# First expert weights loaded slot by slot through SyncE's queue, rectification moved to ScalarE

## The reference

```python
x = L0_attn_x
x = x + _L0_attn_ref(_layernorm(x, axis=-1), Wq, Wk, Wv, Wo, bo)
x = x + _L0_ffn_ref(_layernorm(x, axis=-1), gate_w, w1, b1, w2, b2)

def _L0_ffn_ref(x, gate_w, w1, b1, w2, b2):
    logits = x_flat @ gate_w.T
    probs = jax.nn.softmax(logits / TEMPERATURE, axis=-1)
    topk_probs, topk_idx = jax.lax.top_k(probs, TOPK)          # TOPK = 2
    hidden = jax.nn.relu(jnp.einsum('th,ehf->tef', x_flat, w1) + b1[None])
    all_out = jnp.einsum('tef,efh->teh', hidden, w2) + b2[None]
    gathered = jnp.take_along_axis(all_out, topk_idx[:, :, None], axis=1)
    y_flat = jnp.sum(gathered * topk_probs[:, :, None], axis=1)
```

## Time and profile before

| | us |
|---|---|
| median of 3 runs | 551.57 |
| lowest, highest | 549.81, 553.23 |
| the profiled execution's own time | 548.82 |
| its span, first to last instruction | 547.0 |
| its mean granted TensorE clock | 0.958 |

### The profile page before, as it was taken

The page is one execution under the profiler, slowest core; times in us unless marked ns, Lnnn a source line. Parts: engine busy times, 40 slices in busy tenths (PEclk is TensorE's granted clock), DMA queues, the critical chain, the costliest instruction groups (busy, mean ns, idle before and its releaser), DMA issues.

```text
span 547.0 us, 14291 instructions
## 1 busy us (share of the span) xinstructions
PE 473.8 (87%) x4081; PEld 328.4 (60%) x4081; DVE 415.6 (76%) x1538; ACT 361.6 (66%) x786; POOL 288.5 (53%) x583
## 2 busy tenths in 40 slices
PE   2788999999999999999998899868977889998880
PEld 1534556645546545545545455337867789998870
DVE  5888788998888988988979889725767445556784
ACT  8564877767867867867866668745663467776640
POOL 4512444454766755765765755673454555553441
PEclk9857999999999999999999999998997999999995
DMA  7333233233243243243233236621122222227353
GB/s 217 111 92 107 83 86 103 65 103 98 69 117 102 70 119 105 65 122 103 66 120 101 71 100 168 181 74 51 55 69 69 79 65 71 70 71 253 96 151 96
DMA packets 49741, 54.92 MB, mean 100 GB/s; under 512 B 6851, under 2 KB 41841, under 8 KB 49664
## 3 DMA queue, kind: packets, MB, share of 16 engines
q1 hardware_dynamic: 45312, 45.44, 29.5%
q0 software_dynamic: 4320, 8.47, 4.5%
q10 hardware_dynamic: 32, 0.10, 0.0%
HBM read 34.96 MB, written 17.90 MB: 97 GB/s over the span
## 4 chain that ended last, share of the span: by engine, by line
PE 48%; DVE 29%; issue 8%; ACT 5%; DMA 4%; another core or an unknown queue 2%; SPq 1%; POOL 1%; DVEq 0%; ACTq 0%; POOLq 0%
PE psO L991 11%; DVE psS L1300 11%; PE psS L961 7%; PE psT L1149 7%; DVE maxs L1303 6%; PE psM L1160 5%; PE psO L1160 4%; PE psT L974 3%; PE psS L1149 2%; DVE maxs L1300 2%; PE psS L1139 1%; DMA xs_t<-sorted_x 1%; DVE xn L1230 1%; PE psS L964 1%
## 5 line engine op out<-in xcount | busy, mean ns | idle before, releaser
L774 ACT ACTIVATE PT<-psT 128x512 f32<-128x512 f32 x320 | 172.6, 594 | 71.7 <-PE psO L991 47.0
L1300 DVE CUSTOM_DVE_ANT_0 psS<-mask_row,psS 128x512 f32<-128x512 bf16 (+1 forms) x256 | 157.0, 626 | 36.1 <-PE psS L961 32.8
L961 PE MATMUL psS<-Ks,Qs 96*128 96x128 bf16 (+3 forms) x512 | 135.7, 314 | 13.5 <-DVE maxs L1303 7.5
L581 POOL TENSOR_SCALAR_AFFINE_SELECT PT<-PT 128x512 f32<-128x512 f32 x128 | 79.3, 634 | 106.2 <-ACT PT L774 105.1
L659 POOL DMA_INDIRECT token_y<-Qs,y_row x71 | 70.8, 997 | 83.8 <-DVE Qs L1638 49.7
L974 PE MATMUL psT<-Qs,Ks 108*128 108x384 bf16 (+3 forms) x512 | 110.2, 302 | 3.5 <-ACT PT L774 2.7
L961 PEld LDWEIGHTS psS<-Ks,Qs 96*128 96x128 bf16 x512 | 50.8, 100 | 60.7 <-DVE maxs L1303 24.6
L991 PE MATMUL psO<-PT,Vs 128*32 128x512 f32 (+3 forms) x1024 | 76.0, 436 | 0.9 <-DVE x_all L1326 0.7
L608 POOL DMA_INDIRECT sorted_x<-xn,place x64 | 64.0, 999 | 18.8 <-issue 17.2
L1303 DVE TENSOR_REDUCE maxs<-psS 128x2 f32<-128x512 f32 (+1 forms) x96 | 62.9, 682 | 2.2 <-PE psS L964 1.4
L858 ACT ACTIVATE krest<-psT,turned 128x128 f32<-128x128 f32 x142 | 44.2, 363 | 30.4 <-PE psT L1149 12.0
(11 more groups left out here) (255 smaller groups left out, 744.8 us busy)
## 6 DMA issues: line engine op xcount, KB each, us to landing
Qs<-q_parts SPq DMA_DIRECT2D x96, 96.0 KB
Ks<-k_parts SPq DMA_DIRECT2D x95, 96.0 KB
xs_t<-sorted_x SPq DMA_DIRECT2D x71, 65.0 KB
w_sb<-in_L_ffn_w SPq DMA_DIRECT2D x16, 256.0 KB
q_parts<-qparts SPq DMA_DIRECT2D x32, 96.0 KB, 2.4
k_parts<-kparts SPq DMA_DIRECT2D x8, 384.0 KB, 2.6
x_all<-in_L_attn_x SPq DMA_DIRECT2D x8, 256.0 KB, 4.6
v_all<-token_y SPq DMA_DIRECT2D x4, 512.0 KB, 4.2
```

What stands on the lines that cost most here:

```text
L581: pool.affine_select(out=square, in_=square, compare_op=ALU.is_ge, fill=0.0, base=0, pattern=[[0, GH], [1, P]], channel_multiplier=-1).the ...
L774: act.activation(PT[:, n * T:(n + 1) * T], psT[:, bank, :], ACT.Exp).then_inc(prob_done[bank], 1)
L961: last = pe.matmul(psS[:, bank, c0:c0 + n], Qs[0:QK_ROWS, g, h, j * P:n], Ks[0:QK_ROWS, g, h, 0:n], start=True, stop=alone)
L1300: dve.tensor_tensor_reduce(src, mask_row[:, (CH - 1 - j) * P:], src, 1.0, NEG, ALU.add, ALU.max, maxs[:, par, j, h:h + 1]).then_inc(scores ...
```

## The change

- `load_w1(i, at)` is new on SyncE. It loads 128 x 512 of w1 for slot i from the input in device memory straight to the slot's buffer, 256 KB, once `h_ready` shows that the slot that had the buffer was expanded. SyncE gets an `expert_reader` of its own. The loop issues it for slot i+5, ahead of the load of xs for slot i+6.
- `w1_t` is a ring of four: two halves of `qrest` and the two of `xn`. `w1_sb` and its 8 loads during attention are gone, and `moe_in` counts 9 DMAs instead of 17. `expand(i)` waits for the slot's own `w1_loaded` instead of ScalarE's `w1_copied`.
- `copy_w1` on ScalarE is gone. ScalarE rectifies all four pieces of a slot. VectorE's `relu` is gone.
- From slot 26 on SyncE waits for the second routing (`routed` at 2) before a w1 load.
- The stores of finished batches come one slot later, at slots 57, 60, 63, 66 and 69.

```diff
-STORES = [SLOT_ENDS[0] + 9, SLOT_ENDS[0] + 12, SLOT_ENDS[0] + 15, SLOT_ENDS[0] + 18, SLOT_ENDS[0] + 21]
+STORES = [SLOT_ENDS[0] + 10 + 3 * b for b in range(SORTED[0])]
...
-        w1_sb = sb("w1_sb", [P, E, F])
...
-        w1_t = qrest
+        w1_t = [qrest[:, 0, :], qrest[:, 1, :]] + [xn[:, n, :, :].rearrange("p c d -> p (c d)") for n in range(2)]
...
             def load_experts(experts):
                 for e in experts:
-                    sp.dma_start(w1_sb[:, e:e + 1, :].rearrange("p a f -> p (a f)"), w1[e]).then_inc(moe_in, 16)
...
+            def load_w1(i, at):
+
+                at_least(sp, h_ready, i - ROUND + 1)
+                sp.dma_start(w1_t[i % ROUND], w1[bass.ds(expert_of(i, at), 1), :, :].rearrange("a d f -> d (a f)"))\
+                    .then_inc(w1_loaded[i % ROUND], 16)
...
-            for i in range(AHEAD):
+            expert_of = expert_reader(sp)
+            for i in range(ROUND):
                 load(i)
+                load_w1(i, 0)
+            load(ROUND)
+            load_w1(ROUND, 0)
+            load(ROUND + 1)
             stored = 0
             for i in range(NSLOTS):
+                if i + ROUND + 1 < NSLOTS:
+                    if (i + 2) // ROUND == ROUNDS0[1]:
+                        sp.wait_ge(routed, 2)
+                    load_w1(i + ROUND + 1, i + 2)
                 if i + AHEAD < NSLOTS:
                     load(i + AHEAD)
...
-            def copy_w1(i, e):
-
-                at_least(act, h_ready, i - 1)
-                act.activation(w1_t[:, i % 2, :], w1_sb[:, bass.ds(e, 1), :].rearrange("p a f -> p (a f)"), ACT.Copy)\
-                    .then_inc(w1_copied, 1)
-
             def relu(i, e):
 
                 act.wait_ge(h_ready, i + 1)
                 at_least(act, y_ready, i - 1)
-                for c in range(FC // 2):
-                    last = act.activation(hT[:, i % 2, c * P:(c + 1) * P], banks[2 * (i % 2)][:, c * P:(c + 1) * P], ACT.Relu,
+                for c in range(FC):
+                    bank, c0 = banks[2 * (i % 2) + c // (FC // 2)], c % (FC // 2) * P
+                    last = act.activation(hT[:, i % 2, c * P:(c + 1) * P], bank[:, c0:c0 + P], ACT.Relu,
                                           bias=b1T[:, bass.ds(e * FC + c, 1)])
-                last.then_inc(relu_act, 1)
+                last.then_inc(relu_done, 1)
...
                 pe.wait_ge(xsT_copied, i + 1)
-                pe.wait_ge(w1_copied, i + 1)
-                at_least(pe, relu_act, i - 1)
-                at_least(pe, relu_dve, i - 1)
+                pe.wait_ge(w1_loaded[i % ROUND], (i // ROUND + 1) * 16)
+                at_least(pe, relu_done, i - 1)
...
-            def relu(i, e):
-
-                dve.wait_ge(h_ready, i + 1)
-                at_least(dve, y_ready, i - 1)
-                for c in range(FC // 2, FC):
-                    c0 = (c - FC // 2) * P
-                    last = dve.tensor_scalar(hT[:, i % 2, c * P:(c + 1) * P], banks[2 * (i % 2) + 1][:, c0:c0 + P],
-                                             b1T[:, bass.ds(e * FC + c, 1)], 0.0, ALU.add, ALU.max)
-                last.then_inc(relu_dve, 1)
```

More of the change, by code:

```diff
@@ L313, in layer @@
         results_loaded = sems("results_loaded", BATCH)
-        row_found, xs_loaded = sem("row_found"), sems("xs_loaded", ROUND)
-        xs_turned, xsT_copied, w1_copied, h_ready, relu_act, relu_dve, y_ready, y_copied = (
-            sem(n) for n in ("xs_turned", "xsT_copied", "w1_copied", "h_ready", "relu_act", "relu_dve", "y_ready", "y_copied"))
+        row_found, xs_loaded, w1_loaded = sem("row_found"), sems("xs_loaded", ROUND), sems("w1_loaded", ROUND)
+        xs_turned, xsT_copied, h_ready, relu_done, y_ready, y_copied = (
+            sem(n) for n in ("xs_turned", "xsT_copied", "h_ready", "relu_done", "y_ready", "y_copied"))
         y_scattered = sems("y_scattered", Y_RING)
@@ L856, in relu @@
                 at_least(act, y_ready, i - 1)
-                for c in range(FC // 2):
-                    last = act.activation(hT[:, i % 2, c * P:(c + 1) * P], banks[2 * (i % 2)][:, c * P:(c + 1) * P], ACT.Relu,
+                for c in range(FC):
+                    bank, c0 = banks[2 * (i % 2) + c // (FC // 2)], c % (FC // 2) * P
+                    last = act.activation(hT[:, i % 2, c * P:(c + 1) * P], bank[:, c0:c0 + P], ACT.Relu,
                                           bias=b1T[:, bass.ds(e * FC + c, 1)])
-                last.then_inc(relu_act, 1)
-            act.wait_ge(moe_in, (1 + 2 * E) * 16)
+                last.then_inc(relu_done, 1)
             act.wait_ge(routed, 1)
-            for i in range(2):
-                copy_w1(i, expert_of(i, 0))
             for c in range(CH):
@@ L872, in _ @@
             copy_xs(2)
-            copy_w1(2, expert_of(2, 0))
             for i in range(NSLOTS):
@@ L880, in _ @@
                     copy_xs(i + 3)
-                    copy_w1(i + 3, expert_of(i + 3, i))
                 if i == TAIL["copy_attention"]:
@@ L1143, in expand @@
                 pe.wait_ge(xsT_copied, i + 1)
-                pe.wait_ge(w1_copied, i + 1)
-                at_least(pe, relu_act, i - 1)
-                at_least(pe, relu_dve, i - 1)
+                pe.wait_ge(w1_loaded[i % ROUND], (i // ROUND + 1) * 16)
+                at_least(pe, relu_done, i - 1)
                 for c in range(FC):
                     bank, c0 = banks[2 * (i % 2) + c // (FC // 2)], c % (FC // 2) * P
-                    last = pe.matmul(bank[:, c0:c0 + P], w1_t[:, i % 2, c * P:(c + 1) * P], xsT[:, i % 2, :],
+                    last = pe.matmul(bank[:, c0:c0 + P], w1_t[i % ROUND][:, c * P:(c + 1) * P], xsT[:, i % 2, :],
                                      start=True, stop=True)
@@ L1155, in contract @@
                     pe.wait_ge(heads_copied, STEPS)
-                pe.wait_ge(relu_act, i + 1)
-                pe.wait_ge(relu_dve, i + 1)
+                pe.wait_ge(relu_done, i + 1)
                 at_least(pe, y_copied, i - 1)
@@ L1163, in contract @@
                 last.then_inc(y_ready, 1)
-            pe.wait_ge(moe_in, (1 + 2 * E) * 16)
+            pe.wait_ge(moe_in, (1 + E) * 16)
             pe.wait_ge(routed, 1)
@@ L1709, in tail @@
                     weights()
-            dve.wait_ge(moe_in, (1 + 2 * E) * 16)
+            dve.wait_ge(moe_in, (1 + E) * 16)
             dve.wait_ge(routed, 1)
@@ L1714, in _ @@
             find_rows(1)
-            relu(0, expert_of(0, 0))
             summed = 0
@@ L1719, in _ @@
                     dve.wait_ge(routed, 2)
-                if i + 1 < NSLOTS:
-                    relu(i + 1, expert_of(i + 1, i))
                 copy_y(i, expert_of(i, i))
```

## The result

| | before | after |
|---|---|---|
| median of 4 runs each, us | 550.69 | 561.94 |
| lowest, highest | 549.44, 553.23 | 559.16, 562.90 |
| the profiled execution's own time (span) | 548.82 (547.0) | 562.90 (561.1) |
| mean granted TensorE clock in it | 0.958 | 0.945 |

The ratio is 1.0183, 95% interval 1.0153 to 1.0212: the change makes the kernel 1.8% slower, 11 us by the medians. The prediction said 554.2 and "within 1%". The time is inside its range (542 to 565), but the loss is past the bound of 1%.

A forecast was written before the change was run, and what follows sets the result against it. VectorE's other work mostly stretches slots TensorE could do in 1.90 us; after the change SyncE, at 2.01, sets the pace. Plus 4.6 from contraction 13 to 70, minus 2.0 before, is plus 2.6 on 551.57: 554.2 us, range 542 to 565.

The forecast's parts named there:

- SyncE's pace eats the gain: Expert slots: SyncE needs 2.01 us a slot against TensorE's 1.90; main forecast, within 1%, chance 0.40, range 548 to 559.5.
- the stretch before contraction 13: First expert slots: SyncE isn't the bound; VectorE's relief 2.6 less ScalarE's 0.6 gains 2.0 us.
- SyncE keeps up: Rival, expert slots: SyncE needs only 1.88 us a slot, VectorE's relief counts nearly whole: 541 us, chance 0.22.
- The w1 load, 0.71: SyncE, each slot: decoding 0.13, MOVE 0.06, issue 0.42 and gaps, together 0.71 us, without the register load.
- What else stands in SyncE's queue: SyncE beside its slot loads: eight clears 8.6 us, five result loads 3.0, four stores 1.9.
- hold-ups: Slot loop: behind single GpSimd scatters all sequencers seem to crawl; about 7 us on SyncE today, 8 charged after.
- VectorE's relief: Expert stage: 142 rectifications removed from VectorE, worth 14.6 us if nothing replaces it, 11 net if SyncE isn't the bound.
- The first loads in a new order: Start of the expert stage: costed at nothing, covered by TensorE's wait until 371.77; up to 2 us late otherwise.
- ScalarE's chain: Expert slots: four rectifications on ScalarE take 1.14 us, hidden by 0.12 us; 0.6 us charged in all.
- the gone w1 loads: Attention, 328 to 348 us: eight w1 loads removed, costed at nothing, a gain of 1 us at most.
- SyncE's price is higher: Rival, SyncE in expert slots: 0.85 us a w1 load instead of 0.71, 7.4 us more: 561.6 us, chance 0.26.
- The transfers starve TensorE: Rival, five slots with result loads: DMA makes them 3.5 instead of 2.6 us, 4.5 more: 558.7 us, chance 0.12.

The follow-up runs named there:

- e9: The changed kernel, unedited, run again on a chip where the kernel before takes 551.39 us: 562.56 us, ratio 1.0184.
- e15: The changed kernel, unedited, on a calm chip where the kernel before takes 524.87 us: 533.13 us, ratio 1.0155.
- e16: The kernel before with a memset between the nine back-to-back token scatters at the expert stage's start, calm chip, repeat run: 524.80 us, ratio 1.0012.
- e2: The changed kernel without w1 loads in the slots (fixed w1), with one or two unused register loads on SyncE in their place: 559.22 us, ratio 1.0173.
- e14: The changed kernel without GpSimd's stores of the results of slots 10 to 25, calm chip, repeat run: 530.49 us, ratio 1.0118 to the kernel before.
- e6: The changed kernel without GpSimd's stores of the results of slots 10 to 25, calm chip, first run: 533.18 us, ratio 1.0145 to the kernel before.
- e1: The changed kernel without w1 loads in the slots; all w1 loaded during attention, slot i reads expert i mod 8: 547.50 us against 551.91, ratio 0.9924.
- e8: The changed kernel, but w1_sb is back and VectorE copies w1 into the ring three slots ahead: 518.67 us against 524.81, ratio 0.9877.
- e4: The kernel before plus the change's w1 loads on SyncE into an unused buffer, with one extra wait each: 569.56 us, ratio 1.0324.
- e3: The changed kernel, but each w1 load brings 128 of 512 columns, 64 KB instead of 256: 559.58 us, ratio 1.0168 to the kernel before.
- e10: The changed kernel, but w1 loads read expert i mod 8 at a fixed address, without decoding or register load: 550.65 us against 551.39, ratio 1.0000.
- e12: The changed kernel with VectorE copying w1 from w1_sb and the eight clears spread over slots 13 to 26: 547.59 us against 551.39, ratio 0.9904.
- e11: The change's w1 loads issued from ScalarE instead of its w1 copy, rectifications shared as before: 556.38 us against 551.39, ratio 1.0061.
- e5: The kernel before without GpSimd's stores of the results of slots 10 to 25, calm chip: 525.02 us against 524.81, ratio 1.0001.
- e7: The kernel before with a memset between the nine token scatters at the expert stage's start, calm chip, first run: 525.74 us, ratio 1.0018.
- e13: The kernel before without GpSimd's stores of the results of slots 10 to 25, calm chip, repeat run: 524.64 us, ratio 0.9994.
- e17: The changed kernel with w1 loads at a fixed address (expert i mod 8), repeated on a calm chip: 523.56 us against 524.58, ratio 0.9983.

## Why the prediction was wrong, step by step

The mechanism was right: SyncE's pace eats the gain. Two terms failed. The time of SyncE's queue between contractions 13 and 70 was forecast at 134.7 us and measured 139.5 (144.2 in e9); what it had too low is not the w1 load but what else stands in the queue. And the stretch before contraction 13, forecast 2.0 us shorter, came out 2.0 longer.

**What the change runs into: right.** SyncE became the bound. In the profile of e15, on a chip without crawling, it waits some 3 us in 124, where e16 has 33 us of waits in 112. Waits of SyncE, 388 to 512 us in e15, then 388 to 500 in e16, which is the kernel before but for the spread burst:

```profile
SPq L453 <- PE psS L1143: 1.8, 6, 0.6
SPq L121 <- DVE y_row L1636: 1.0, 1, 1.0
```

```profile
SPq L121 <- DVE y_row L1647: 33.2, 41, 2.4
```

The rule of the Trainium skill that was weighed ("DMA: Bandwidth & Descriptors", section "Issuing engines are not separate DMA queues": initiating takes the sequencer little time beside the DMA) was read as "SyncE keeps up", at 541. What the Trainium skill states there is so here: an issue takes 0.333 us, and the load lands 3.2 us after it began. The reading doesn't follow from it: with a w1 load issued every 1.94 us and landing 3.2 us later the loads overlap, while their issues and register work stand one behind the other on SyncE, and e2, which moves not one w1 byte in the slots, still loses 1.7%.

**The w1 load, 0.71: too high, not too low.** SyncE's issues in e15 (start, us):

```profile
413.81 0.33 SPq L459 DMA_DIRECT2D xn<-in_L_ffn_w  x1
415.00 0.33 SPq L454 DMA_DIRECT2D xs_t<-sorted_x  x1
416.20 0.33 SPq L459 DMA_DIRECT2D xn<-in_L_ffn_w  x1
417.38 0.33 SPq L454 DMA_DIRECT2D xs_t<-sorted_x  x1
418.00 0.33 SPq L459 DMA_DIRECT2D qrest<-in_L_ffn_w  x1
419.17 0.33 SPq L454 DMA_DIRECT2D xs_t<-sorted_x  x1
419.79 0.33 SPq L459 DMA_DIRECT2D qrest<-in_L_ffn_w  x1
```

418.00 to 419.79 is 1.79 for a slot without the register load, 413.81 to 416.20 is 2.39 for one with it; one in four has it, so 1.94 on average, where the prediction had 2.01. With xs at 1.16 the load is 0.63. The register arithmetic is 0.14 (expected 0.13), the issue 0.333, which is the lower bound of the 0.34 to 0.51 and not the middle. Its records in e15 (ns min/median/max, first and last start):

```profile
L459 SPq FUSED_REGOPS  x57: 91/140/149, 380.0 to 511.4; - x57
L459 SPq DMA_DIRECT2D qrest<-in_L_ffn_w x28: 332/333/1495, 384.6 to 509.5; - x28
DMA to landing us min/median/max: 2.6/3.2/5.6
```

The landing, costed at 3.0, is 3.2.

**What else stands in SyncE's queue: too low.** From the issue of w1 load 18 to that of load 70, 52 iterations, the prediction's terms give 118.0 (104.5 + 8.6 + 3.0 + 1.9) and 8 of hold-ups, 126.0. Without crawling it is 123.4 in e15, the same kernel, and 121.2 and 120.2 in e14 and e6, which lack 16 stores; with it, 131.5 in the kernel after and 132.9 in e9. By the same kernel the hold-ups are 8 to 9.5, as expected, and the plain part is 5.4 above the 118.0 although a slot is cheaper than thought; with e14 and e6 taken in (mean 121.6) it is 10 and 3.6. The clears are part of it:

```profile
394.74 0.40 SPq L459 DMA_DIRECT2D qrest<-in_L_ffn_w  x1
395.98 0.33 SPq L454 DMA_DIRECT2D xs_t<-sorted_x  x1
397.08 0.36 SPq L406 DMA_DIRECT2D sorted_x<-pad_row  x1
397.73 0.33 SPq L459 DMA_DIRECT2D qrest<-in_L_ffn_w  x1
```

A slot with a clear is 2.99, or 1.20 above 1.79; w1 loads 18 to 25 take 23.9 us, and 23.5 and 23.2 in e14 and e6; less seven slots at 1.94 that is 9.6 to 10.3 for the eight clears instead of 8.6. Result loads and stores are about 6 instead of 4.9 (loads 56 to 70: 33.4 less 14 slots at 1.94 is 6.2). The largest part lies between them: loads 26 to 56 take 64.4 us, 6.2 more than 30 slots at 1.94. And three w1 issues of e15, two of them in that stretch and one behind it, take 1.3 to 1.5 us instead of 0.333, 3.2 us more together, which no row of before could show. What the other 4 us of that stretch went to was not traced. In all, contraction 13 to 70 took 139.5 us instead of 134.7: a term mis-sized by 4.8. On SyncE's own count it is 5.5 (131.5 less 126.0), by the comparison with e15 all but 0.1 of it plain work.

**VectorE's relief, 14.6, or 11 net: too high.** Net, it is 4.4 us by e1, 6.1 by e8, 8 by e4 against the change. The prediction took a slot in which VectorE rectified over 0.5 us after ScalarE for one that VectorE had made long. On the chips at 525 us the kernel before needs 120.3 us for these 57 slots (e16, outputs 13 to 70: 388.93 to 509.2) and not 129.3 (output to output in the profile of before): 9 of the 22 us above TensorE's pace are not there on a calm chip. That crawling made VectorE late in them, so that relief can't give them back, is argued from this and not shown. In the same stretch before has TensorE's clock at half level for 6.8 us (412.5 to 419.3), e16 not at all; and between 357 and 533 us it is at half level for 20.4 us in e1 and 10.2 in the kernel before, which may hide some of e1's gain. In this sum the error changed nothing, since SyncE's pace replaced these slots altogether; it did flatter the rival "SyncE keeps up". At 541 that was out of reach: e1, which has no w1 work in the slots, takes 547.5.

**Before contraction 13: −2.0 forecast, +2.0 measured.** This is the second step that failed, and only on the chips at 551 us. On a calm one it is right: from the last exponentials to contraction 13 it is 33.6 us in e15 against 35.65 in e16, −2.1. In the kernel after the relief is there too: outputs 2 to 13 take 24.1 us instead of 27.3. But outputs 0 to 2 take 8.4 us instead of 4.2 (375.3 to 383.7, against 372.8 to 377.0). On a calm chip they take 5.1 in e15 against 4.7 in e16.

"The first loads in a new order" were costed at nothing. It is not that TensorE waited for one of them: slots 0 and 1 were expanded early, and ScalarE rectified them late. Timeline of the kernel after:

```profile
362.27 1.12 PE L1152 MATMUL psT<-turned,qrest 128*128 128x128 f32 x8
...
363.78 0.61 PE L1152 MATMUL psS<-turned,qrest 128*128 128x128 f32 x4
...
366.57 1.14 ACT L867 ACTIVATE krest<-psT,turned 128x128 f32<-128x128 f32 x4 [3.82 <-remote]
...
372.03 0.96 POOL L622 DMA_INDIRECT sorted_x<-xn,place  x1 [0.30 <-issue]
...
375.20 0.62 ACT L867 ACTIVATE krest<-psT,turned 128x128 f32<-128x128 f32 x2 [7.12 <-remote]
```

GpSimd's burst of scatters ends at 372.99, and slot 1 is rectified from 375.20 on, 2.2 us later; in the kernel before it is 0.1 us sooner than the burst's end (370.64 against 370.75). It is 2.2 to 3.4 us later in all runs on such chips that issue w1 loads from SyncE (e3, e4, e9, and e10, whose loads have no decoding), and at most 0.1 later in e1, e2 and e12, which have none; in e11, where ScalarE issues them, it is 1.5. So the added loads go with the delay and their decoding isn't needed for it; how they make ScalarE see its semaphore late is open. Eight of the 35 lengthened records lie there too, between 365 and 374 us. And TensorE, after 4.69 us of waiting, does slots 1 and 2 at half clock, from 375.9 to 382.7 us; in the kernel before the half level lasts there from 371.5 to 374.9. The prediction, which knew the record of the earlier trace rows, charged crawling only behind contraction 13. The size is uncertain: in e9 contraction 13 comes 45.8 us behind the last exponentials, +0.8 and not +2.0.

**ScalarE's chain, 0.6, and the gone w1 loads, nothing: not contradicted.** In e8, on a calm chip, ScalarE does all four rectifications and TensorE waits 1.4 us for one in the whole stage; in e1 it waits 12.8 us in six waits, in the kernel before 12.6 in five. For the gone loads see attention above: what the kernel after is behind at 325 us it is behind at its end.

**The sum.** Forecast +2.6; 4.8 more for SyncE's pace, 4.0 for the start (−2.0 to +2.0) and 0.5 at the end make +11.9. The profiles differ by 14.1, 2.2 of it in attention, which leaves 11.9. The medians differ by 11.3. That the parts fit so well is one pair of executions; in e9 nearly all of it is in the slots. On a calm chip the start gives its 2.0 back and the slots cost more against their own base: contraction 13 to 70 takes 133.2 us in e15 and 120.3 in e16, in an execution of e15 that was 3.1 us above its median.

**The rivals.** "SyncE's price is higher" gave 561.6, the right time by luck: the load itself is cheaper than forecast, its neighbours and the start are dearer. "The transfers starve TensorE" put 4.5 us on five slots; e3 leaves at most about that for three quarters of the bytes over the whole stage (its middle is under 1 us by the ratios, 3.5 by the medians). "SyncE keeps up" had its sum wrong: 2.01 less 0.13 for decoding and 0.08 for the issue is 1.80, not 1.88. The forecast of 0.4 for "within 1%" rested on a SyncE at 2.01 against 1.90, with every extra item on its queue taken at the price of a quiet record.

## What to carry to other kernels

Draw up a time budget for a queue that only issues DMAs as for an engine: register load, arithmetic and issue of every DMA in it, at the lengths of the sequencer's records. What the view of waits shows it to wait for in the kernel before (here 50 us in 180) is an upper bound on what a change may add to it; 0.78 us more in each of 71 slots (0.63 for the load, 0.15 for its share of register loads) is 55 us and used that up, and then each clear and result load was paid in full.

Before a long slot is put down to the engine that was late in it, ask what made that engine late: if the register records around it are lengthened too, the slot may not get shorter by giving the engine less work. And take a second profile of the same kernel before an effect of 2 us in one stretch is given a cause: two of the changed kernel differ by 4.7 us in the slots alone.

## What the runs showed of the hardware

- The same program takes 525 us on three of the chips and 551 us on the others. On the first SyncE has none to one lengthened register record between 350 and 560 us in the kernel before's variants (e5, e7, e13, e16), on the second 9 in the kernel before. From the last exponentials of attention to output 0 it is 7.2 us (e16) against 15.6 in the kernel before. Most of the lengthened records (27 of 35 in the kernel after, 7 of 9 before) come with the second of two indirect DMAs of GpSimd about 1.3 us apart, or right behind it. Such pairs alone don't make them: e15 has as many and 4 lengthened records. Whether they are needed for it wasn't tested, since the runs that part the pairs all fell on calm chips.
- A w1 issue with a register address was shorter than one with a fixed address for the same 128 x 512 tile: a median of 0.333 us in e15, 0.432 in e17 and e10, and 0.508 for the loads during attention.
- One to three of the 71 w1 issues of a profile take 1.0 to 1.9 us (436.8, 451.9 and 492.4 us in e15); their cause is open.
